# Cross-attention context loaded in 32 by 32 blocks and transposed by VectorE instead of TensorE

## What is computed

```python
q = (x @ Wq + bq).reshape(b, lq, H, D)        # x: 16 x 256 x 128
k = (embeds @ Wk + bk).reshape(b, lk, H, D)   # embeds (ctx_1024): 16 x 1601 x 128
v = (embeds @ Wv + bv).reshape(b, lk, H, D)
scores = jnp.einsum('bqhd,bkhd->bhqk', q, k) * SCALE
attn = jax.nn.softmax(scores, axis=-1)
ctx = jnp.einsum('bhqk,bkhd->bqhd', attn, v).reshape(b, lq, AD)
return ctx @ Wo + bo
```

## Time and profile before

| | |
|---|---|
| median of 3 runs | 2809.16 us (2807.8 to 2810.15) |
| the profiled execution | 2807.67 us, its span 2805.9 us |
| busy | PE 2706.7 us (96%), DVE 2064.5 (74%), ACT 1719.6 (61%), POOL 2158.7 (77%) |
| granted TensorE clock, mean | 0.982 of 2.4 GHz |
| DMA | 55.54 MB, mean 20 GB/s |

### The profile page before, as it was taken

How to read it: one execution, slowest core, us unless ns; L and a number is a source line. 1 busy time by engine, 2 the same in 40 slices (tenths; PEclk the granted TensorE clock), 3 DMA queues, 4 the chain that set the end, 5 groups by cost and what they waited for, 6 DMA issues and landing times.

```text
span 2805.9 us, 71012 instructions
## 1 busy us (share of the span) xinstructions
PE 2706.7 (96%) x28404; PEld 2300.6 (82%) x28404; DVE 2064.5 (74%) x4265; ACT 1719.6 (61%) x3445; POOL 2158.7 (77%) x1758
## 2 busy tenths in 40 slices
PE   5699999999999999999999999999999999999967
PEld 3588888888888888888888888888888888888845
DVE  7677777777877777777777777777777777777723
ACT  2366666666666666666666666666666666666612
POOL 2287888888788788878788888878878787878845
PEclk9699999999999999999999999999999999999979
DMA  2300000000000000000000000000000000000030
GB/s 75 76 8 21 9 21 11 8 25 7 23 9 23 9 13 20 9 23 9 21 11 21 11 7 25 7 23 9 23 9 14 18 9 22 9 9 10 9 96 27
DMA packets 85319, 55.54 MB, mean 20 GB/s; under 512 B 14367, under 2 KB 82677, under 8 KB 84992
## 3 DMA queue, kind: packets, MB, share of 16 engines
q1 hardware_dynamic: 82944, 47.38, 6.1%
q0 software_dynamic: 2048, 3.66, 0.4%
HBM read 42.86 MB, written 8.72 MB: 18 GB/s over the span
## 4 chain that ended last, share of the span: by engine, by line
PE 93%; issue 3%; POOL 2%; DVE 1%; ACT 1%; DMA 0%; POOLq 0%; SPq 0%; DVEq 0%; ACTq 0%
PE ps L1378 27%; PE ps L1409 25%; PE ps L1368 8%; PE ps L1359 4%; PE ps L1361 4%; PE ps L1360 4%; PE ps L1343 3%; PE ps L1344 3%; PE ps L1345 3%; PE ps L1418 3%; PE ps L1350 2%; PE ps L1427 2%; PE ps L1542 1%; PE ps L1533 1%; PE ps L1332 1%
## 5 line engine op out<-in xcount | busy, mean ns | idle before, releaser
L616 POOL TENSOR_TENSOR key_sums<-key_sums,prob_T 128x512 f32<-128x512 f32 (+1 forms) x1408 | 1812.9, 1288 | 161.5 <-POOL key_sums L616 1.4
L1044 DVE TENSOR_REDUCE mx<-ps 128x1 f32<-128x400 f32 (+1 forms) x2048 | 1062.1, 570 | 335.8 <-PE ps L1368 282.0
L806 ACT ACTIVATE prob_T<-ps 128x512 f32<-128x512 f32 x1536 | 834.3, 596 | 104.3 <-PE ps L1378 58.8
L1378 PE MATMUL ps<-shift,shift_w 64*128 64x256 f32 (+1 forms) x3328 | 767.3, 281 | 5.7 <-ACT shift L777 5.7
L1378 PE MATMUL ps<-q_hi,k_hi 64*128 64x256 f32 (+1 forms) x3328 | 760.7, 283 | 0.0
L1378 PE MATMUL ps<-q_lo,k_hi 64*128 64x256 f32 (+1 forms) x3328 | 741.9, 278 | 0.0
L1409 PE MATMUL ps<-prob_T,v_sb 128*64 128x256 f32 (+1 forms) x6656 | 740.4, 379 | 0.7 <-ACT prob_T L806 0.7
L1378 PE MATMUL ps<-q_hi,k_lo 64*128 64x256 f32 (+1 forms) x3328 | 739.8, 277 | 0.0
L1409 PEld LDWEIGHTS ps<-prob_T,v_sb 128*64 128x64 f32 (+1 forms) x6656 | 478.4, 137 | 241.1 <-ACT prob_T L806 1.1
L1378 PEld LDWEIGHTS ps<-shift,shift_w 64*128 64x128 f32 (+1 forms) x3328 | 571.9, 180 | 55.0 <-issue 55.0
L1378 PEld LDWEIGHTS ps<-q_hi,k_hi 64*128 64x128 f32 (+1 forms) x3328 | 548.7, 181 | 6.4 <-ACT prob_T L806 0.6
(11 more groups left out here) (172 smaller groups left out, 3507.6 us busy)
## 6 DMA issues: line engine op xcount, KB each, us to landing
shift_f<-row_shifts SPq DMA_DIRECT2D x256, 64.0 KB, 2.6
ctx_raw<-in_ctx_dram SPq DMA_DIRECT2D x16, 768.0 KB
row_shifts<-nm_T SPq DMA_DIRECT2D x512, 0.5 KB
prob_T<-in_L_ffn_W_dram SPq DMA_DIRECT2D x12, 256.0 KB, 5.3
slots_in<-no_row SPq DMA_DIRECT2D x1, 2080.0 KB, 16.1
v_sb<-slots_in SPq DMA_DIRECT2D x8, 260.0 KB, 5.0
xs<-in_x_dram SPq DMA_DIRECT2D x8, 256.0 KB, 3.0
xres<-in_x_dram SPq DMA_DIRECT2D x8, 256.0 KB, 2.8
```

The lines of the kernel that those rows point to most:

```text
L616: op = nc.gpsimd.tensor_tensor(acc[0:rows, :, :], acc[0:rows, :, :], prob_T[0:rows, :, k, :], ALU.add)
L806: nc.scalar.activation(prob_T[:, h, 2 * i - 2:2 * i, :].rearrange("p k t -> p (k t)"), ps[:, bank, :], ACT.Exp).then_inc(ring_act, 1)
L1044: v.tensor_reduce(mx[:, qt, h, c:c + 1], ps[:, at.bank("mx", r, c, qt, h), 0:WID[c]], AX.X, ALU.max).then_inc(ring_dve, 1)
L1378: return mm(ps[0:rows, bank, n * T:n * T + T], keys_part, query_part[lanes, :], start=(step == 0), stop=(step == 3))
```

## The change

The context is loaded in blocks. Each of ten DMAs a batch brings 32 channels and half of the 50 blocks of 32 keys into 32 partitions of `ctx_raw` (rows of 128 bytes; two small ones bring the last key). VectorE transposes 32 by 32 blocks, in four instructions (three of 512 columns and one of 96), into a new SBUF tile `ctx_T`; ScalarE and VectorE make the high and low parts from `ctx_T` instead of PSUM. TensorE's transposes and their four ring fills go. VectorE transposes the next batch's context at the end of pairs 2 (first chunk), 3 (second) and 4 (third and fourth). ScalarE's four casts stay in pair 5. Of the low part, chunks 0 and 1 are made in pair 5, chunks 2 (512 columns) and 3 (66) in pair 6 between the maxima and the keys; TensorE waits for the first two before the values and keys of pair 6, and for all four in their middle. SyncE issues the pieces of a batch in pairs 6 and 7 of the batch two before it and pairs 0 and 1 of the batch one before; the first batch's ten are issued by ScalarE in the setup, behind the casts of `wk_hi` and `wv_hi`. The `ranks` matmuls and `place` move from pair 6 to pair 7. The ternary weights' buffers move into memory that is free in the setup.

```diff
-ROUTE_PAIRS = {1: ("dve", "out"), 3: ("act", "x2t"), 4: ("dve", "logits"), 6: ("dve", "ranks")}
+ROUTE_PAIRS = {1: ("dve", "out"), 3: ("act", "x2t"), 4: ("dve", "logits"), 7: ("dve", "ranks")}
...
+        def load_context(eng, b, piece):
+
+            if piece < 8:
+                half, j = piece // 4, piece % 4
+                k0, n = half * (BLOCKS // 2), BLOCKS // 2
+                src = C_IN[b * KEYS + 32 * k0:b * KEYS + 32 * (k0 + n), 32 * j:32 * j + 32]
+                dst = ctx_raw[32 * j:32 * j + 32, 32 * k0:32 * (k0 + n)]
+                eng.dma_start(dst.rearrange("i (k c) -> i k c", c=32), src.rearrange("(k i) c -> i k c", i=32))\
+                    .then_inc(ctx_in, 16)
...
+                    if s >= 6 and at.b + 2 < B:
+                        later_context(at, at.b + 2, s - 6)
+                    if s < 2 and 0 < at.b < B - 1:
+                        later_context(at, at.b + 1, s + 2)
...
+            act.wait_ge(ctx_clear, 1)
+            for piece in range(PIECES):
+                load_context(act, 0, piece)
+
             act.wait_ge(setup_tr, 1)
...
+            def context_high(b, c):
+                k0, k1 = TURN_CHUNKS[c]
+                act.wait_ge(ctx_turned, b * 4 + c + 1)
+                copy(ctx_hi[:, k0:min(k1, KPAD)], ctx_T[:, k0:min(k1, KPAD)]).then_inc(ctx_hi_ok, 1)
...
+            def context_turned(b, c):
+
+                if c == 0:
+                    dve.wait_ge(ctx_in, (b + 1) * PIECES * 16)
+
+                wait(dve, ctx_lo_ok, b * 4)
+                k0, k1 = TURN_CHUNKS[c]
+                v.transpose(ctx_T[:, k0:k1], ctx_raw[:, k0:k1]).then_inc(ctx_turned, 1)
+
+            def context_low(b, c):
                 dve.wait_ge(ctx_hi_ok, b * 4 + c + 1)
-                v.tensor_tensor(ctx_lo[:, k0:k0 + n], ps[:, at.bank("ctx", r, c), 0:n],
-                                ctx_hi[:, k0:k0 + n].bitcast(F32), ALU.subtract).then_inc(ring_dve, 1)
+                cols = slice(TURN_CHUNKS[c][0], min(TURN_CHUNKS[c][1], KPAD))
+                v.tensor_tensor(ctx_lo[:, cols], ctx_T[:, cols], ctx_hi[:, cols].bitcast(F32), ALU.subtract)\
+                    .then_inc(ctx_lo_ok, 1)
...
+                    if s == 6 and more:
+                        context_low(at.b + 1, 2)
+                        context_low(at.b + 1, 3)
                     for c in range(4):
                         if after:
                             keys_low(at, s + 2, c)
...
                     if s == 5 and more:
-                        for c in range(4):
-                            context_low(at, NJ, at.b + 1, c)
+                        context_low(at.b + 1, 0)
+                        context_low(at.b + 1, 1)
...
+                    if 2 <= s < 5 and more:
+                        for c in ((0,), (1,), (2, 3))[s - 2]:
+                            context_turned(at.b + 1, c)
...
-            def context(at, r, b, c):
-                if c == 0:
-                    pe.wait_ge(ctx_in, b * 48 + 48)
-                bank = bank_of(at, "ctx", r, c)
-                for n, k in enumerate(K_CHUNKS[c]):
-                    rows = P if k < KT - 1 else KREM + 1
-                    last = tr(ps[:, bank, n * P:n * P + rows], ctx_raw[0:rows, k, :], ident[0:rows, 0:rows])
-                last.then_inc(ring_full, 1)
...
                     if s == 6 and more:
-                        context_read(at, NJ)
+                        context_read(at.b + 1, 2)
                     some = value_fills(s) if after else []
                     for i in range(4):
+                        if s == 6 and more and i == 2:
+                            context_read(at.b + 1, 4)
```

More of the change, by code:

```diff
@@ L122, in batch_fills @@
             put(*ROUTE_PAIRS[s], -1)
-        if s == 5 and more:
-            for c in range(4):
-                put("dve", "ctx", 8, c)
         if s > 0 or kind != "first":
@@ L231, in decoder_layer @@
     KPAD = KEYS + 1
+    assert KEYS // 32 % 2 == 0
     assert KT == 2 * (UNITS - 1) + 1 and NJ == SLOTS_A_BATCH
-    K_CHUNKS = [list(range(4 * c, min(4 * c + 4, KT))) for c in range(4)]
+    BLOCKS = KEYS // 32
+    assert KEYS == 32 * BLOCKS + 1
+    TURNED = 32 * (BLOCKS + 1)
+    TURN_CHUNKS = [(c * 512, min(c * 512 + 512, TURNED)) for c in range(4)]
+    PIECES = 10
     NPAIRS = B * NJ
@@ L341, in decoder_layer @@
         wq_rows, wk_rows, wv_rows = (spare[:, n * AD:(n + 1) * AD] for n in range(3))
+        w_rows, w_tmp, w_tern = (spare[:, 3 * AD + n * 4 * P:3 * AD + (n + 1) * 4 * P].rearrange("p (m n) -> p m n", n=P)
+                                 for n in range(3))
         EW = F + FC * P
@@ L450, in decoder_layer @@
         block = stack.enter_context(nc.Block())
+        def load_context(eng, b, piece):
[6 more added lines that the diff above has]
+                    .then_inc(ctx_in, 16)
+            else:
+                row = b * KEYS + KEYS - 1
+                eng.dma_start(ctx_raw[piece - 8:P:32, 32 * BLOCKS:TURNED],
+                              C_IN[row:row + 1].rearrange("a (j c) -> (a j) c", c=32)).then_inc(ctx_in, 16)
         @block.sync
@@ L523, in store_dropped, with later_context @@
                 sp.dma_start(out[b].rearrange("(t p) d -> p t d", p=P), out_rows).then_inc(o_out, 16)
-            def next_context(at):
-                sp.wait_ge(ctx_hi_ok, at.b * 4 + 8)
-                load_context(at.b + 2)
-            load_context(0)
-            sp.wait_ge(ctx_hi_ok, 4)
-            load_context(1)
+            def later_context(at, b, part):
+                if part == 0:
+                    sp.wait_ge(ctx_turned, 4 * b)
+                for piece in range(part * 2, part * 2 + 2) if part < 3 else range(6, PIECES):
+                    load_context(sp, b, piece)
+            sp.wait_ge(ctx_turned, 4)
+            for piece in range(PIECES):
+                load_context(sp, 1, piece)
             sp.wait_ge(consts_ready, 2)
@@ L539, in _ @@
                 batch(Batch("mid", b, B))
-            at = Batch("mid", B - 2, B)
-            for s in range(NJ):
-                turn_shift(at, s + 1)
-                if s == 5:
-                    store_dropped(B - 3)
+            batch(Batch("mid", B - 2, B))
             at = Batch("last", B - 1, B)
@@ L745, in _ @@
             keep_x1T(AB - 1)
-            def context_high(at, r, n_batches, c):
-                tiles = K_CHUNKS[c]
-                n = sum(P if k < KT - 1 else KREM + 1 for k in tiles)
-                act.wait_ge(ring_full, at.full("ctx", r, c))
-                copy(ctx_hi[:, tiles[0] * P:tiles[0] * P + n], ps[:, at.bank("ctx", r, c), 0:n]).then_inc(ctx_hi_ok, 1)
+            def context_high(b, c):
+                k0, k1 = TURN_CHUNKS[c]
+                act.wait_ge(ctx_turned, b * 4 + c + 1)
+                copy(ctx_hi[:, k0:min(k1, KPAD)], ctx_T[:, k0:min(k1, KPAD)]).then_inc(ctx_hi_ok, 1)
             def keys_high(at, r, c):
@@ L1189, in _ @@
             for c in range(4):
-                context_low(at, 0, 0, c)
+                context_turned(0, c)
+            for c in range(4):
+                context_low(0, c)
             for c in range(4):
@@ L1324, in bank_of, with context_read @@
                 return banks_of(at, key)[0]
[L1326 to L1338 removed]
+            def context_read(b, chunks):
+                pe.wait_ge(ctx_lo_ok, b * 4 + chunks)
             def keys(at, r, c):
@@ L1483, in batch @@
                             route_logits(at)
-                        if s == 6:
+                        if s == 7:
                             ranks(at, at.b - 1)
-                    if s == 5 and more:
-                        for c in range(4):
-                            context(at, NJ, at.b + 1, c)
                     if s > 0 or at.kind != "first":
@@ L1493, in _ @@
             at = Batch("start", 0, B)
-            for c in range(4):
-                context(at, 0, 0, c)
-            context_read(at, 0)
+            context_read(0, 4)
             for c in range(4):
```

33 lines of the change are left out of this document (9 added, 24 removed).

## The result

| | time in us | ratio to the kernel before, 95% interval |
|---|---|---|
| before | 2807.64 (2806.75 to 2810.15, 6 runs) | |
| changed | 2818.64 (2817.33 to 2819.08, 6 runs) | 1.0037 [1.0024, 1.0050] |

The change makes the kernel slower by 11.0 us, 0.39%. The profiled execution took 2818.71 us (span 2816.9) against 2807.67 (span 2805.9). The forecast was 2811, no change that can be told, with 2804 to 2818 as its own range; the result lies just above that, inside the whole range with the rivals (2790 to 2822), on the slower side, which had a chance of 0.34.

What follows compares the result with a forecast made beforehand. TensorE, holding 93% of the chain, was taken as the bound. Terms summed from the profiled execution: 2807.7 − 20.9 + 21.5 + 4.2 − 1.8 = 2810.7, about 2811 us; own range 2804 to 2818, with rivals 2790 to 2822.

Steps and rivals of the forecast that it cites:

- TensorE's transposes: The 13 context transposes leave TensorE's pair 5: 1.39 us a batch in 15 batches, −20.9 us.
- VectorE's transposes: At the end of pairs 2 to 4: 0.71 us for 512 columns, 0.28 for 96, mostly covered, cost 0.
- The stall in pair 6: TensorE waits behind the second keys for VectorE's low-part subtractions: 1.43 us in 15 batches, +21.5 us.
- Rival 1: In pair 6 VectorE keeps the ports through both subtractions: stall 0.35 us, time 2794.5 us, chance 0.20.
- The first half in pair 5: Two low-part subtractions reading SBUF replace four in pair 5: counted 0, up to 0.5 us a batch on the upper side.
- rival 4: VectorE falls behind in pairs 5 and 6: 0.3 to 0.8 us a batch more, 2815 to 2823 us, chance 0.05.
- The issues on ScalarE: In the setup, ten load issues ahead of the copy to `w_T` take 5.6 us: +4.2 us.
- Rival 2: Setup issues on ScalarE are dear, the ten over 8.2 us: 2813.3 us, up to 2822; chance 0.15.
- The first context: Ahead of the attention, the first batch's context is ready sooner and TensorE's first keys start earlier: −1.8 us.
- The row shift: The first row shift, ahead of the first pair; its being late was named a sign that the prediction is wrong.
- rival 3: Rows of 128 bytes make loads slow; the first shift waits about 10 us, time 2821 us, chance 0.05.
- `ranks` and `place`: Moved from pair 6 to pair 7: the same work in another pair, cost 0.

Runs made afterwards that it cites:

- experiment 5: Changed kernel with 11 of GpSimd's 12 additions of a pair cut to one column each, only for timing: 2786.94 us (one run).
- experiment 2: Changed kernel with pair 6's two subtractions (512 and 66 columns) made by one instruction of 578 columns: 2801.49 us, ratio 0.9975.
- experiment 7: Changed kernel with the first batch's loads on SyncE and the whole low part in one 1602-column subtraction in pair 5: 2797.78 us, ratio 0.9964.
- Experiments 3 and 4: Changed kernel with the 66-column subtraction moved from pair 6 to pair 5: 2813.56 us; with all four subtractions in pair 5: 2824.05 us.
- experiment 10: On top of experiment 6, `ranks` and `place` moved back to pair 6: 2808.19 us on a slower chip, ratio 0.9942 to the kernel before.
- experiment 1: Changed kernel with the first batch's ten loads issued by SyncE behind the first token load, instead of by ScalarE: 2811.76 us, ratio 1.0011.
- the last three experiments: On a slower chip: SyncE loads with 1536 columns in pair 5 and 66 in pair 6, 0.9941; experiment 10; 578 columns with ScalarE loads behind `w_T` copy, 0.9932.
- experiment 6: Changed kernel with the first batch's loads on SyncE and one subtraction of 578 columns in pair 6: 2794.13 us, ratio 0.9952.

## Why the prediction was right, and where it was off

The forecast mechanism held, and the result is within its range, but not because the sum was close. The profiled execution took 2818.7 us against a sum of 2810.7, and the forecast of no change is missed by a change of 11 us. Of the 8.0 us between the two, 2.3 are the setup, the one term that was badly mis-sized, 1.2 the stall, 0.6 the transposes and 0.1 the first context; 3.8 us lie in stretches for which the sum had no term. It is the width of the range, made for the rivals, that took this in.

**TensorE's transposes** were put at 1.39 us a batch and measured 1.35 less: -20.3 instead of -20.9. **VectorE's transposes** took 0.70 us for 512 columns (predicted 0.71) and 0.23 for 96 (0.28), and cost TensorE nothing. **The stall in pair 6** was put at 1.43 us and measured 1.51 (21.24 against 19.73), +22.7 instead of +21.5. The prediction's own working ends at 1.46 (264.65 to 266.11), and it gives no reason for taking 1.43. The cause of the stall is shown: additions cut, 0 (experiment 5); one instruction instead of two, 0.4 (experiment 2). Rival 1, that VectorE keeps the ports through both steps, is refuted by the trace itself, where an addition ran between them.

The rule of the Trainium skill, page "SBUF — State Buffer" (section "Who interferes with whom"), that whoever starts first has the shared ports for its whole instruction and the other fully blocks, agrees with the rows on the stall of pair 6 and with those of experiment 7: by it the 2.74 us addition stood still for 1.61 us, from 407.54 to 409.15, and did its work in the 1.13 behind that. Alone, or beside work that it does not collide with, an addition takes 1.30, so up to 0.17 us of it would have gone ahead of the wait.

**The first half in pair 5** was counted at nothing, and it cost nothing, but its cover was used up to the end: the two subtractions took 2.7 us and VectorE's idle time of 1.91 us ahead of the maxima of pair 6 is gone. Experiments 3 and 4 show what comes next: `heads_T`, `heads_raw`, a bank. The prediction had the idle time right and did not name that chain; rival 4 named only late maxima.

**The issues on ScalarE** are the step that failed, and it is a size: I put 5.6 us for ten and +4.2 for the setup; they took 9.6 us from 10.30 and the setup lost 6.54. Two things were off. A big issue took 0.99 us on the mean instead of 0.62, and a small one 0.82 instead of 0.3. Against that the first were issued while the casts still ran, which the sum did not have. Rival 2 is what happened, at its lower end: its condition holds (9.6 us for the ten, over 8.2; 0.99 for a big one, over 0.95), while the loss of 6.54 is a little under the 6.8 that went with it.

**The first context** saved 1.68 us (predicted 1.8). **The row shift** was not late: the cast of the first one began at 142.91 and ended 0.14 us ahead of the first pair, as before, so rival 3 (slow loads) did not happen. **`ranks` and `place`** cost 0, shown by experiment 10.

These terms make -20.3 + 22.7 + 6.5 - 1.7 = +7.2 us. The other 3.8 were not in the sum: the recurrence is 1.4 us longer, the way from the first keys to the first pair 0.9, the end of the program 1.4. For the first I have a reading, not a proof. These are the stretches in which TensorE's granted clock changes between its two levels. The recurrence before (25.66 to 106.62), in the changed kernel, and in experiment 1, whole stretch with busy time of PE, PEld, DVE, ACT, POOL, clock, DMA share:

```profile
25.66:106.62 80.96, 56.74 (x237) 36.57 (x237) 61.00 (x193) 21.93 (x39) 29.89 (x23) 0.77 0.20 59
```

```profile
32.20:114.57 82.37, 58.82 (x237) 37.91 (x237) 61.06 (x193) 21.90 (x39) 29.84 (x23) 0.79 0.16 48
```

```profile
25.55:108.12 82.57, 60.53 (x237) 39.01 (x237) 61.08 (x193) 21.92 (x39) 29.83 (x23) 0.73 0.16 48
```

The same 237 matmuls took 56.74, 58.82 and 60.53 us, while VectorE's and ScalarE's work took the same. TensorE was at 1.2 GHz, the lower of its two levels, for more of them: a mean of 0.77 before is about 37 us at the lower level, and 0.73 in experiment 1 about 45 (estimates from these rows). In the changed kernel the record of the clock begins only at 39 us, so its 0.79 is too high. Behind the attention the output projection of the last batch, 32 matmuls in both kernels, shows the same, before and changed:

```profile
2697.20:2702.40 5.20, 5.17 (x32) 4.98 (x32) 0.31 (x1) 0.00 (x0) 0.00 (x0) 0.73 1.06 326
```

```profile
2706.70:2712.90 6.20, 6.15 (x32) 5.96 (x32) 0.29 (x1) 0.00 (x0) 0.00 (x0) 0.61 1.05 341
```

That is 0.98 us of the 1.4 at the end of the program, at a granted clock of 0.61 instead of 0.73. So 1 to 3 us of a difference between two of these kernels can hang on when the clock moves. No run holds the clock fixed, so why it moved at other moments stays open, and the link to the 3.8 us is argued.

## What to carry to other kernels

When VectorE instructions with two SBUF inputs run beside a steady stream of GpSimd instructions, count them before you count their columns: here each cost one wait for the running one, and GpSimd got in at every border between two that was looked at. Merge them, up to the point where the merged one must wait for its last input or makes VectorE late for what stands behind it.

DMA issues are work of the engine that issues them. Ten of them in front of one copy cost 6.5 us; behind that copy, or on SyncE, they did not delay the setup. Before moving a load onto an engine's queue, look for the idle time on that queue that comes next.

A gain on the busiest engine (1.35 us a batch) is worth little if its price is a wait of that same engine for the one that took the work over.

## What the runs showed of the hardware that I had not expected

The same eight big issues took 7.9 us on ScalarE ahead of the copy (0.40 us the shortest, 2.34 the longest), 5.5 us there 3 us later (longest 1.42), and 5.8 us on SyncE. Each of the three has one to three of over 1.1 us in its middle. SyncE's own issues ran beside the first until about 13 us, but the longest came at 14.9; what made them long stays open.

On the chip of the last three experiments the kernel before took 16.5 us more. In their traces pair 0 of the middle batches is 20.45 to 20.71 long instead of 19.73, while the other pairs agree with those of experiment 6 to 0.03 us, but for the edits. The traces put part of it down to waits of TensorE for ScalarE's exponentials, which experiment 6 does not have at this place. One batch of experiment 10, TensorE, ScalarE and VectorE:

```profile
1577.62 0.38 PE L1399 MATMUL ps<-shift,shift_w 64*128 64x256 f32 x1 [0.55 <-ACT prob_T L819]
...
1576.96 2.07 ACT L819 ACTIVATE prob_T<-ps 128x512 f32<-128x512 f32 x4 [1.22 <-PE ps L1399]
...
1576.95 2.02 DVE L1066 TENSOR_REDUCE mx<-ps 128x1 f32<-128x400 f32 x4 [1.11 <-PE ps L1399]
```

ScalarE and VectorE go on at the same moment, after over a microsecond of idle time, while TensorE's matmuls had started without a pause until 1576.78; then TensorE must wait for ScalarE. What held both up together is not shown, nor why only on this chip.
